# A recurrence between two expert FFNs: beats of up to five steps, copies moved to ScalarE, another bank and another plan

## The chip, the cores and the metric

The kernel runs on one core of a Trainium2 chip. The metric is the device time of one execution in microseconds (us). The core has a matmul engine (TensorE, PE in the profile; PEld is its weight load), VectorE (DVE), ScalarE (ACT), GpSimd (POOL) and a queue engine (SyncE, SP) that issues most of the plain DMAs. GpSimd issues the indirect DMAs.

## The reference

Input x is 16 sequences of 512 tokens of 128 numbers, float32. Three stages, each with a residual:

```python
x = x + 0.5 * ffn(layernorm(x), router_w, expert_fc, expert_proj)
x = x + rnn(layernorm(x), Wi, bi, Wh, bh)
x = x + 0.5 * ffn(layernorm(x), router_w, expert_fc, expert_proj)
```

`rnn` is a recurrence over the 512 tokens of each sequence: h = tanh(xi[t] + h @ Wh.T + bh), with xi = x @ Wi.T + bi. `ffn` sends every token to one of 8 experts, the argmax of its 8 logits; the expert computes square(relu(x @ fc)) @ proj.T with 512 hidden units.

## The kernel before, in words

**Units, tiles, steps.** The 512 time steps are cut into 16 units of 32 (UNIT). A unit has 512 tokens, 4 rows of 128 (UR). Both FFNs gather tokens by expert into tiles of 128 tokens. The first FFN has two groups (FIRST = [4, 12] units): 23 tiles and 55 tiles. The second FFN has one pool of 71 tiles, which is filled in stages of SECOND = [7, 3, 3, 1, 1, 1] units; a tile can be loaded when its stage is routed and scattered, and the last 18 of the 71 wait for the last stage. A step t needs state t-1 (`step`, L1632, two 16-column matmuls on PE; `tanh`, L1441, on ACT), so the 512 steps are one chain.

**One tile.** Its rows arrive in `xs_sb` (`fetch`, an indirect DMA of POOL at L1085, in the first FFN; `load`, SP, L968, in the second), its expert's weights in `w_sb` (`weights`, SP, L980). PE transposes it (`turn_x`, L1600), ACT copies the result (`copy_x`, L1456), PE makes the hidden units in two halves of four matmuls (`product1`, L1609), DVE applies relu (`relu`, L1334), ACT squares in two halves (`square`, L1449), PE multiplies back in two halves (`product2`, L1622) into the bank `yp`. DVE takes it from there in `finish`: a plain copy in the first FFN (L1344), a scaled addition in the second (L1341). Results of the first FFN go to DRAM (`store`, SP, L985) and come back row by row (`gather`, POOL, L1110); those of the second are put in place by POOL (`put`, L1116). After each indirect DMA POOL clears a small buffer (L1137).

**Unit by unit.** What a unit needs before its steps: `gather` 4 rows, `add_back` (L1352), statistics (L1161, L1165), a root on POOL (L1058, L1061), `normalise` (L1184), a transposition `turn2` on PE whose result ACT evacuates (L1472), `inputs` (`xi`, L1591) into bank z[u % 2], `add_bias` (L1359). After its steps: `hadd` (a transposition that DVE adds up, L1364), `turn` (a transposition that ACT evacuates), `logits` (L1547). A stage then has `pick`, `rank` (L1559), `place` and `list` on DVE and PE, and its rows are scattered to DRAM by POOL (`scatter`, L1094).

**Routing of the first FFN.** For each group `logits`, `pick`, `rank`, `slots`; then a list of tokens is made by matmuls of one-hot matrices (`hot` by DVE or POOL, L1073; `index`, L1580) and copied out (`table`, L1287). The bank of group 0 is z[0], that of group 1 is z[1]; therefore `xi` of unit 0 waits for table 0 and `xi` of unit 1 for table 1.

**The order of the work.** Nothing is decided on the chip: `plan` simulates the kernel in Python with costs and arrival times written in it (ARRIVE, PR) and writes a list of beats. A beat has at most one tile in each of its three phases (transposition of the next, first product of the present, second product of the last), up to BEAT = 4 steps, up to two turns, and side work on PE and DVE. Each engine runs its part of the beats in this fixed order. On PE a beat is: step 0, turn_x, first half of product 1, first turn, step 1, second half of product 1, half of logits or xi, step 2, half of product 2, second turn, step 3, the other half of product 2, the other half of logits or xi, then rank and index. On ACT: tanh 0, square, tanh 1, square, evacuation of the first turn, tanh 2, copy_x, tanh 3, evacuation of the second turn. When a beat has no tile, PE fills up with matmuls whose result nobody reads (`keep_warm`, L1637).

`centre` (8 products at the start, L1530) subtracts the mean from the experts' first weights; ACT writes the result back and SP stores it to `fc_dram`, from which all tiles' weights come.

## Time and profile before

| | us |
|---|---|
| median of 3 runs | 615.17 |
| lowest and highest of them | 611.65, 615.24 |
| the profiled execution's own time | 610.88 |
| its span, first to last instruction | 609.2 |
| PE busy in the span | 557.5 |
| ACT busy in the span | 232.0 |

The span is what the profile divides up; the time of the same execution is 1.7 us longer. The profile's busy PE includes the matmuls of `keep_warm`.

### The profile page before, as it was taken

What the parts mean: (1) busy time and instruction counts of PE and PEld (TensorE: products, weight loads), DVE (VectorE), ACT (ScalarE), POOL (GpSimd) and SP (SyncE); (2) the same over time, 40 slices, a digit from 0 to 9 for tenths busy, and PEclk for the clock granted to TensorE, in tenths of its full rate; (3) what the DMA queues carried; (4) which work ended last, traced back from release to release, by engine and by line L of the source; (5) the groups of instructions that cost most, each with busy time, mean ns of one, the idle gap of its engine ahead of it and who ended that gap; (6) DMA issues with size and microseconds to landing.
All of it is one profiled execution on the core that took longest, in us unless ns stands there. A gap on an engine that the chain in (4) does not pass through costs nothing.

```text
span 609.2 us, 14909 instructions
## 1 busy us (share of the span) xinstructions
PE 557.5 (92%) x4503; PEld 521.0 (86%) x4503; DVE 338.7 (56%) x1169; ACT 232.0 (38%) x950; POOL 443.4 (73%) x637
## 2 busy tenths in 40 slices
PE   7978979979999999999999999899999899997992
PEld 6677877979999899998998888889999899896991
DVE  3617889565564455545468511645647774675550
ACT  1203321334445444454442433344454444433440
POOL 3486089887756878887857898877774878778672
PEclk9997999999999999999999999999999999999997
DMA  7976850254434444444411013544343354445740
GB/s 278 400 247 201 257 170 7 39 176 137 142 112 139 124 135 132 141 127 120 110 41 58 31 41 101 162 127 135 123 140 113 99 149 153 123 152 159 222 129 1
DMA packets 58476, 83.07 MB, mean 136 GB/s; under 512 B 10031, under 2 KB 30386, under 8 KB 57888
## 3 DMA queue, kind: packets, MB, share of 16 engines
q1 hardware_dynamic: 49392, 64.20, 33.2%
q0 software_dynamic: 8864, 17.78, 10.1%
q8 instruction: 40, 0.66, 0.4%
q14 instruction: 36, 0.29, 0.2%
q10 hardware_dynamic: 144, 0.14, 0.1%
HBM read 65.81 MB, written 16.72 MB: 135 GB/s over the span
## 4 chain that ended last, share of the span: by engine, by line
PE 71%; DVE 10%; issue 7%; POOL 5%; DMA 2%; ACT 2%; SPq 1%; ACTq 1%; POOLq 0%; DVEq 0%
PE yp L1622 20%; PE hp L1609 16%; PE z L1632 14%; PE hp L1637 7%; PE mT L1508 4%; POOL out_dram L1116 3%; PE xTp L1600 2%; PE lg L1547 2%; PE z L1591 2%; PE z L1580 2%; DVE r_sb L1334 1%; POOL hot L1073 1%; DMA hsT<-in_x_rows_dram 1%; PE z L1547 1%; DVE stats L1161 1%
## 5 line engine op out<-in xcount | busy, mean ns | idle before, releaser
L1622 PE MATMUL yp<-projT,s_sb 128*128 x1192 | 192.0, 292 | 23.0 <-DVE y_sb L1344 7.6
L1441 ACT ACTIVATE hsT<-z 128x16 f32<-128x16 f32 x512 | 93.8, 183 | 242.2 <-PE z L1632 181.3
L1609 PE MATMUL hp<-xT_sb,w_sb 128*128 128x128 f32 x1192 | 182.7, 283 | 0.5 <-ACT xT_sb L1456 0.5
L1632 PEld LDWEIGHTS z<-hsT,w_all 128*128 128x128 f32 x1024 | 155.3, 190 | 29.5 <-ACT hsT L1441 7.2
L1622 PEld LDWEIGHTS yp<-projT,s_sb 128*128 128x128 f32 x1192 | 154.3, 193 | 27.9 <-issue 27.5
L1334 DVE TENSOR_SCALAR r_sb<-hp 128x512 f32<-128x512 f32 x149 | 102.7, 689 | 120.8 <-PE hp L1609 87.4
L1632 PE MATMUL z<-hsT,w_all 128*128 128x16 f32 x1024 | 159.9, 232 | 7.2 <-ACT hsT L1441 4.9
L1609 PEld LDWEIGHTS hp<-xT_sb,w_sb 128*128 128x128 f32 x1192 | 157.0, 195 | 1.0 <-ACT xT_sb L1456 0.7
L1449 ACT ACTIVATE s_sb<-r_sb 128x256 f32<-128x256 f32 (+1 forms) x247 | 112.0, 454 | 75.1 <-issue 45.6
L1137 POOL MEMSET idle<- 128x400 f32 x277 | 125.2, 452 | 0.2
L1110 POOL DMA_INDIRECT back<-ys_dram,pos x64 | 62.0, 969 | 49.3 <-DMA ys_dram<-y_sb 23.8
L1116 POOL DMA_INDIRECT out_dram<-y_sb,xs_sb x71 | 69.6, 980 | 29.9 <-issue 17.2
L1085 POOL DMA_INDIRECT xs_sb<-in_x_rows_dram,index x78 | 75.8, 972 | 15.3 <-issue 11.5
L1094 POOL DMA_INDIRECT xs_dram<-pay,pos x64 | 62.7, 979 | 21.7 <-DVE pos L1297 12.0
L1637 PE MATMUL hp<-w_all,ident 128*128 128x256 f32 x178 | 59.1, 418 | 0.0
L1456 ACT ACTIVATE xT_sb<-xTp 128x128 f32<-128x128 f32 x149 | 40.5, 272 | 16.9 <-issue 9.7
L1600 PE MATMUL xTp<-ident,xs_sb 128*128 128x128 f32 x149 | 44.4, 298 | 0.5 <-ACT xT_sb L1456 0.5
L1344 DVE COPY y_sb<-yp 128x128 f32<-128x128 f32 x78 | 22.1, 283 | 25.2 <-PE yp L1622 20.6
L1341 DVE SCALAR_TENSOR_TENSOR y_sb<-yp,xs_sb 128x128 f32<-128x128 f32 x71 | 24.6, 347 | 20.5 <-PE yp L1622 15.5
L1073 POOL TENSOR_SCALAR hot<-kio,slot_f,ids 128x128 f32<-128x128 f32 x28 | 23.8, 860 | 15.4 <-DVE slot_f L1257 15.4
L1600 PEld LDWEIGHTS xTp<-ident,xs_sb 128*128 128x128 f32 x149 | 29.4, 197 | 1.0 <-DMA xs_sb<-xs_dram 1.0
L1161 DVE BATCH_NORM_STATS2 stats<-pay 128x6 f32<-128x128 f32 x128 | 27.7, 280 | 0.5
(154 smaller groups left out, 483.2 us busy)
## 6 DMA issues: line engine op xcount, KB each, us to landing
w_sb<-fc_dram SPq DMA_DIRECT2D x149, 256.0 KB
ys_dram<-y_sb SPq DMA_DIRECT2D x78, 64.0 KB
xs_sb<-xs_dram SPq DMA_DIRECT2D x71, 65.0 KB
hsT<-in_x_rows_dram SPq DMA_DIRECT2D x16, 256.0 KB, 4.3
hsT<-in_x_cols_dram SPq DMA_DIRECT2D x3, 1024.0 KB, 16.3
fc_sb<-in_fc_in_dram SPq DMA_DIRECT2D x4, 512.0 KB, 5.4
projT<-in_proj_in_dram SPq DMA_DIRECT2D x1, 2048.0 KB, 11.6
fc_dram<-fc_sb SPq DMA_DIRECT2D x8, 256.0 KB
```

What stands on the lines that cost most here:

```text
L1085: pool.indirect_dma_start(out=xs_sb[:, g % RING, 0:D], out_offset=None, in_=x_rows.rearrange("p (n d) -> (p n) d", d=D), in_offset=bass.In ...
L1094: pool.indirect_dma_start(out=xs2_dram, in_=pay[:, n, :], in_offset=None, out_offset=bass.IndirectOffsetOnAxis(ap=pos[:, 1, n:n + 1].bitca ...
L1116: pool.indirect_dma_start(out=out.rearrange("b t d -> (b t) d"), in_=y_sb[:, g % RING, :], in_offset=None, out_offset=bass.IndirectOffsetO ...
L1137: pool.memset(idle[:, :], 0.0).then_inc(s_idle, 1)
L1334: dve.tensor_scalar(r_sb[:, g % 2, :], hp[:, g % 2, :], 0.0, None, ALU.max).then_inc(s_relu, 1)
L1441: act.activation(state(t), z_step(t), ACT.Tanh).then_inc(s_h, 1)
L1449: act.activation(s_sb[:, g % 2, half * w:(half + n) * w, :].rearrange("p c t -> p (c t)"), r_sb[:, g % 2, half * w * P:(half + n) * w * P] ...
L1600: pe.transpose(xTp[:, 0:P], xs_sb[:, g % RING, XR:XR + D], ident[:, :]).then_inc(s_tx, 1)
L1609: mm = pe.matmul(hp[:, g % 2, h * P:(h + 1) * P], w_sb[:, g % WRING, h * P:(h + 1) * P], xT_sb[:, g % 2, :], start=True, stop=True)
L1622: mm = pe.matmul(yp[:, 0:D], s_sb[:, g % 2, h, :], projT[:, bass.ds(offsets[g] + h * D, D)], start=(h == 0), stop=(h == HC - 1))
L1632: pe.matmul(z_step(t), WhT, state(t - 1) if t else hsT[:, 0:B], start=False, stop=True, skip_group_check=True).then_inc(s_mm, 1)
L1637: pe.matmul(lg[:, 0:FILL] if early else hp[:, 0, 0:FILL], ident[:, :], w_all[:, 0:FILL], start=True, stop=True)
```

## The change

- BEAT is 5. A fifth step may be in a beat only for steps from PR["from"] = 89.4 to PR["to"] = 402.9; elsewhere a beat has at most four. PE does step 4 after the second half of product 2 and the second half of logits or xi. ACT does tanh 4 as its last tanh.
- Turns move: a lone turn, or the second of two, is now done by PE at the end of the beat behind step 4, and evacuated by ACT as the last thing of the beat; the first of two stands where the second stood.
- The first FFN's copy out of `yp` goes from DVE (`finish`) to ACT (`bring`), behind tanh 3 and copy_x and ahead of tanh 4. There are two semaphores (s_y1, s_y2) in place of s_y, and `made` waits on the one of the tile's kind.
- Group 1 of the first FFN uses the bank `lg`, that the second FFN's logits use; the second FFN's first stage waits for table 1 before its first logits, and `xi` of unit 1 no longer does. The early `keep_warm` writes to the free half of `xTp`.
- `centre` pieces are exempt from the planner's limits on room in a beat, so that they come in a row; the planner takes the first weights as ready 5.2 us after the last of them (4.0 before), and the rows of x as arriving 5 to 5.5 us later.
- SECOND is [7, 1, 1, 3, 1, 1, 1, 1], eight stages for six. The last stage is the same.
- All of the planner's weights (PR) are other numbers, so the order of beats, of SP's queue and of POOL's queue is another.

```diff
-BEAT = 4
+BEAT = 5
-SECOND = [7, 3, 3, 1, 1, 1]
+SECOND = [7, 1, 1, 3, 1, 1, 1, 1]
-          ... "rows": [34.0 + 1.2 * u for u in range(FIRST[0])] + [45.0 + 2.0 * u for u in range(NU - FIRST[0])]}
-PR = {"lat1": 317.13, "lat2": 230.174, "lat3": -30.24, "last": -472.607, "hor": 65.326, "beat": 1.723, "put": -120.179, "dve": 2.508, "act": 0.415, "pe": -0.984, "early": 2.791, "load": 0.767, "hold": -207.944, "late": -122.862, "gather": -278.073, "scatter2": 505.514, "fetch": -278.424, "slack": -26.428}
+          ... "rows": [39.5 + 1.2 * u for u in range(FIRST[0])] + [50.0 + 2.0 * u for u in range(NU - FIRST[0])]}
+PR = {"lat1": 255.575, "lat2": 265.398, "lat3": -19.271, "last": -329.665, "hor": 127.118, "beat": 5.85, "put": -103.734, "dve": 3.048, "act": 4.178, "pe": 0.886, "early": 5.706, "load": -0.726, "hold": -85.01, "late": -170.227, "gather": -260.2, "scatter2": 637.695, "fetch": -55.443, "slack": 59.124, "from": 89.418, "to": 402.858}
...
-            at = max(choice[1], ev["centre", E - 1] + 4.0, ...
+            at = max(choice[1], ev["centre", E - 1] + 5.2, ...
-        while t < T and len(b.steps) < BEAT and ...
+        while t < T and len(b.steps) < (BEAT if PR["from"] <= t < PR["to"] else BEAT - 1) and ...
-                if d_pe and pe_at + d_pe > pe_room and (b.pe or b.turns) or d_act and ...
+                if what != "centre" and d_pe and pe_at + d_pe > pe_room and (b.pe or b.turns) or what != "centre" and d_act and ...
...
-            return lg[:, :] if r.second else z[:, r.index, :]
+            return z[:, 0, :] if r.index == 0 else lg[:, :]
...
+            def bring(g):
+                act.wait_ge(s_m2, g + 1)
+                if g >= RING:
+                    put_landed(act, g - RING)
+                act.activation(y_sb[:, g % RING, :], yp[:, 0:D], ACT.Copy).then_inc(s_y1, 1)
...
                         if last is not None and i < 2:
                             square(last, i, 1)
-                        if i == 1:
-                            if turns[0]:
-                                evacuate(*turns[0])
+                        if i == 3 and len(turns) > 1 and turns[0]:
+                            evacuate(*turns[0])
                         if after is not None and i == 2:
                             copy_x(after)
-                    if turns[1]:
-                        evacuate(*turns[1])
+                        if last is not None and not is_second[last] and i == 3:
+                            bring(last)
+                    if turns and turns[-1]:
+                        evacuate(*turns[-1])
...
-                    if u < len(first):
-                        pe.wait_ge(s_table, table_no[first[u].index])
+                    if u == 0:
+                        pe.wait_ge(s_table, table_no[first[0].index])
...
-                if b.turns:
-                    turn(b.turns[0])
-                elif alone and n > 0:
+                if alone and n > 0:
                     keep_warm()
...
                 if alone and n > 3 and not products:
                     keep_warm()
+                if n > 4:
+                    step(b.steps[4])
+                if b.turns:
+                    turn(b.turns[-1])
+                elif alone and n > 4:
+                    keep_warm()
```

## Rows read from the trace of the kernel before

**Rows 1.** The page, busy time by engine: us, share, instructions.
```profile
PE 557.5 (92%) x4503; PEld 521.0 (86%) x4503; DVE 338.7 (56%) x1169; ACT 232.0 (38%) x950; POOL 443.4 (73%) x637
```

**Rows 2.** Stretch, length, busy PE, PEld, DVE, ACT, POOL; clock, DMA share, GB/s.
```profile
125.30:137.80 12.50, 9.38 (x72) 8.18 (x72) 8.99 (x35) 3.60 (x8) 11.08 (x17) 1.00 0.66 201
137.80:320.00 182.20, 176.37 (x1493) 169.94 (x1493) 95.95 (x316) 85.57 (x384) 136.01 (x195) 1.00 0.41 122
320.00:384.00 64.00, 64.00 (x437) 52.32 (x434) 26.96 (x110) 20.60 (x101) 55.15 (x78) 1.00 0.21 67
384.00:534.80 150.80, 142.10 (x1235) 137.50 (x1236) 91.63 (x295) 68.65 (x312) 114.07 (x161) 1.00 0.42 131
...
562.30:597.20 34.90, 33.92 (x298) 33.52 (x298) 18.40 (x36) 14.09 (x34) 24.23 (x35) 1.00 0.55 163
```

**Rows 3.** Stretch, length, busy (count), clock, DMA: ACT at L1441 alone: one instruction for each step.
```profile
137.80:320.00 182.20, 38.82 (x212) 1.00 0.41 122
320.00:384.00 64.00, 17.04 (x93) 1.00 0.21 67
384.00:534.80 150.80, 32.08 (x175) 1.00 0.42 131
```

**Rows 4.** The same, DVE at L1334 alone: one instruction for each tile.
```profile
137.80:320.00 182.20, 37.21 (x54) 1.00 0.41 122
384.00:534.80 150.80, 30.05 (x44) 1.00 0.42 131
```

**Rows 5.** The same, PE at L1637 alone: the filling matmuls.
```profile
320.00:384.00 64.00, 46.88 (x140) 1.00 0.21 67
```

**Rows 6.** Timeline of ACT, beats with a tile: start, us, instruction, [idle before].
```profile
140.09 0.18 ACT L1441 ACTIVATE hsT<-z 128x16 f32<-128x16 f32 x1 [0.32 <-issue]
140.76 0.18 ACT L1441 ACTIVATE hsT<-z 128x16 f32<-128x16 f32 x1 [0.49 <-PE z L1632]
...
153.62 0.18 ACT L1441 ACTIVATE hsT<-z 128x16 f32<-128x16 f32 x1 [0.52 <-PE z L1632]
...
154.76 0.18 ACT L1441 ACTIVATE hsT<-z 128x16 f32<-128x16 f32 x1 [0.65 <-issue]
...
155.15 0.59 ACT L1472 ACTIVATE xnT<-mT 128x512 f32<-128x512 f32 x1
155.62 0.18 ACT L1441 ACTIVATE hsT<-z 128x16 f32<-128x16 f32 x1
```

**Rows 7.** Timeline of DVE and PE in the same two beats.
```profile
140.69 0.29 DVE L1344 COPY y_sb<-yp 128x128 f32<-128x128 f32 x1 [0.51 <-PE yp L1622]
...
153.99 0.60 PE L1508 MATMUL mT<-ident,xn 128*128 128x128 f32 x4
154.43 0.29 PE L1632 MATMUL z<-hsT,w_all 128*128 128x16 f32 x2
154.57 0.69 PE L1609 MATMUL hp<-xT_sb,w_sb 128*128 128x128 f32 x4
```

**Rows 8.** Timeline of the start: centring, a statistics wait, the first gather.
```profile
18.70 1.02 PE L1530 MATMUL hp<-fc_sb,level 128*128 128x512 f32 x2
...
19.99 1.02 PE L1530 MATMUL hp<-fc_sb,level 128*128 128x512 f32 x2
...
26.91 1.02 PE L1530 MATMUL hp<-fc_sb,level 128*128 128x512 f32 x2
...
44.47 0.87 DVE L1161 BATCH_NORM_STATS2 stats<-hsT 128x6 f32<-128x128 f32 x4 [5.92 <-DMA hsT<-in_x_rows_dram]
...
78.00 0.95 POOL L1110 DMA_INDIRECT back<-ys_dram,pos  x1 [22.18 <-DMA ys_dram<-y_sb]
```

**Rows 9.** Timeline from the last gather of unit 1 to its bias.
```profile
118.86 0.95 POOL L1110 DMA_INDIRECT back<-ys_dram,pos  x1 [0.17 <-issue]
...
136.72 0.76 DVE L1359 TENSOR_SCALAR z<-z,bias 128x512 f32<-128x512 f32 x1 [0.69 <-PE z L1591]
```

**Rows 10.** Timeline of POOL and SP: first scatter of the second FFN, first load.
```profile
323.28 1.02 POOL L1094 DMA_INDIRECT xs_dram<-pay,pos  x1 [2.02 <-DVE pos L1297]
...
374.80 0.30 SPq L968 DMA_DIRECT2D xs_sb<-xs_dram  x1
```

More of the change, by code:

```diff
@@ L365, in possible @@
         if what == "xi":
-            if key < len(first) and ("table", first[key]) not in ev:
+            if key == 0 and ("table", first[0]) not in ev:
                 return None
@@ L470, in on_pe @@
             if alone and n > 3 and not products:
+                warm()
+            if n > 4:
+                yield from step(4)
+            if b.turns:
+                yield from turn(len(b.turns) - 1)
+            elif alone and n > 4:
                 warm()
@@ L506, in evacuate, with bring @@
                     do(0.59, p)
+            def bring():
+                yield ("m2", last), ("free", last - RING) if last >= RING else None
+                do(0.26, ("y", last))
+            by_act = last is not None and order[last][0] is not None
             if n > 0:
@@ L544, in end @@
                 do(0.292, ("y", last))
-            if last is not None and not n:
+            by_dve = last is not None and order[last][0] is None
+            if by_dve and not n:
                 yield from end()
@@ L555, in on_dve @@
                 do(dve_time(p), p)
-            if last is not None and n:
+            if by_dve and n:
                 yield from end()
@@ L594, in plan @@
         after = line.pop(0) if line and ev.get(("load", line[0]), 1e9) <= pe + PR["load"] and ev["w", line[0]] <= pe + PR["load"] + 1.0 else None
-        while t < T and len(b.steps) < BEAT and ev.get(("bias", t // UNIT), 1e9) <= pe + 0.3:
+        while t < T and len(b.steps) < (BEAT if PR["from"] <= t < PR["to"] else BEAT - 1) and ev.get(("bias", t // UNIT), 1e9) <= pe + 0.3:
             b.steps.append(t)
@@ L647, in plan @@
                         lg_after[lg_owner] = lg_last
-                elif what == "place":
+                elif what == "place" or what == "table" and piece[1].index:
                     lg_owner, lg_last = None, piece
@@ L917, in put_landed, with made @@
             engine.wait_ge((s_put if is_second[g] else s_store)[g % RING], 16 * n)
+        def made(engine, g):
+            n = sum(is_second[i] == is_second[g] for i in range(g + 1))
+            engine.wait_ge(s_y2 if is_second[g] else s_y1, n)
         def offset(engine, kind, g):
@@ L1426, in _ @@
                     add_states(*p[1:])
-                if last is not None and not b.steps:
+                if last is not None and is_second[last] and not b.steps:
                     finish(last)
@@ L1430, in _ @@
                     side(p)
-                if last is not None and b.steps:
+                if last is not None and is_second[last] and b.steps:
                     finish(last)
@@ L1475, in _ @@
                 after, last = tile_at(b.at + 1), tile_at(b.at - 1)
[L1476 removed]
+                turns = [p if p[0] != "hadd" else None for p in b.turns]
                 if b.steps:
```

59 lines of the change are left out of this document (32 added, 27 removed).

## The prediction, made before the change was run

> **What bounds the kernel now.** I began with the page's busy times: PE is busy 557.5 of 609.2 us [rows 1], which looks like a kernel bound by PE. The table of stretches says something else [rows 2]. From 320 to 384 us PE is busy all the time, but 46.88 of its 64 us are filling matmuls [rows 5]: there is no tile to work on, and only the recurrence advances. So I cut the span by what the recurrence does, with the count of tanh instructions in each stretch [rows 3].
>
> The chain of steps runs without a break from about 97.6 us to 532.4 us (the last tanh). Its parts: 32 steps up to 125.3; a stop of 12.5 us with no step; 212 steps in 182.2 us (0.86 us each, 54 tiles beside them [rows 4]); 93 steps in 64.0 us (0.69 each, no tile); 175 steps in the next 148.4 us (0.85 each, 44 tiles beside them). After the last step come about 30 us in which the last unit is routed and scattered, 34.9 us for the 18 tiles of the last stage (1.94 us each [rows 2]) and 12.0 us in which the last results land and the program ends. The sum is 97.6 + 27.7 + 12.5 + 182.2 + 64.0 + 148.4 + 76.8 = 609.2, the span. So the end is set by the start of the recurrence, by its steps, and by a tail of 76.8 us that no faster PE shortens, as long as enough tiles are done when the steps end. It is by this sum that I cost the change.
>
> Inside a beat with a tile, tanh follows tanh after 0.67 us (140.09 to 140.76 [rows 6]), and in beats without a tile after 0.69 us on average with all their side work. So a half product of four matmuls between two steps costs the chain nothing: it fills PE while the chain goes through ACT. What costs is everything beyond it. A turn in the first gap makes 1.14 us of one interval and 0.86 of the next (153.62, 154.76, 155.62 [rows 6]), 0.47 + 0.19 = 0.66 us in all. turn_x costs about 0.1 us a tile. Each half of logits or xi costs about what the four matmuls of a turn cost, 0.44 us (153.99 to 154.43 [rows 7]).
>
> **Part by part.**
>
> *Start (to the first step, 97.6 us).* The centring products come every 1.3 us (18.70, 19.99) and then wait; the eighth is at 26.91 [rows 8]. In a row it would come 2.6 us after the sixth, at about 22.6: 4.3 us earlier for the first weights. Their store shares the DMA queues with the first loads and may not gain as much: I take 3. DVE waits 5.92 us for rows of x with the relu of a tile behind it [rows 8]; with the later arrival in the plan these statistics stand later: 2 us. The copies of the first 11 tiles leave DVE (0.29 us each, 0.2 of it not overlapped): 2 us, as the first gather, which waited 22.18 us for stores [rows 8], starts that much earlier. Together 7 us, bounds 0 and 11.
>
> *The stop before unit 1 (12.5 us).* The new bank takes away the wait of `xi` for table 1. But the trace shows that the data was late too: the last gather of unit 1 is issued at 118.86, its bias done at 137.5 [rows 9]. POOL, with hots and fetches in its queue, decides when those gathers come. PR still gives hots precedence. I take half of the stop, 6 us; bounds 0 and 12.5.
>
> *Fifth step and moved turns.* The fifth step makes no step faster by itself: the interval is 0.67 with a half product or without. What changes is the turn. Behind step 4 PE has nothing to do until the state is back, so a turn that DVE evacuates (hadd) costs nothing there: 0.44 us saved. One that ACT evacuates starts 0.14 us after step 4's own matmuls start; the evacuation can start 0.69 later (0.60 of matmuls and the signal) and gives ACT free 0.47 later (155.15 to 155.62), so the next tanh can start 1.30 us after step 4. Without the turn it would start at 0.33 (154.43 to 154.76) + 0.67 = 1.00. Cost 0.30 for 0.66. A unit has one turn of the first and two of the second kind: 0.44 + 2 x 0.36 = 1.2 us saved a unit. In beats of four steps the turn follows a half product: 0.83 for 0.66, 0.34 a unit lost. By my count of steps in the new order, 8.2 units run beside tiles in beats of five and 5.2 in beats of four: -9.8 + 1.8 = -8.0 us. Bounds -12 (the 0.66 wholly gone) and +4 (the plan makes few full beats of five).
>
> *The copy on ACT.* In the trace DVE starts it at 140.69 and the next tanh starts at 140.76 [rows 6, 7]. On ACT I take the 0.29 us that it has on DVE, less the 0.12 by which the next instruction there starts before the end of one (155.15 + 0.59 against 155.62): the tanh would start at 140.86 instead, 0.10 us late. Queued behind the waiting copy are that tanh, hence all later steps, and the evacuation. The 55 tiles of group 1 run beside steps: +5.5 us, the 23 of group 0 mostly do not. Bounds 0 (where logits or xi stand between) and 0.5 us a copy, 27 us: the wait for product 2 then holds a tanh for most of a period.
> The Trainium skill (Perfetto Trace Analysis, Optimizing Scalar/DVE Operations) says that if DVE is saturated, work may be moved to ScalarE. The trace does not show DVE saturated: DVE is busy 56% over the span, and ACT, at 38% [rows 1], is the engine that the chain passes through; by the rule alone the 55 copies would be a gain, by the rows they cost 5.5 us.
>
> *Fewer tiles a step, and the scatter.* With five steps to a tile, step 224, which opens the first stage of seven units, comes with about 42 instead of 48 of the 55 tiles done, and the remaining 13 fill part of the 51.5 us that the 28 scatters and the rest of POOL's queue take from 323.28 to the first load at 374.80 [rows 10]. The stretch without tiles shrinks from 64 to some 35 us. For the chain this is no gain: the same 95 or so tiles are done before it ends, and 1.3 units more run beside tiles, where their side work is not free (0.6 for turns and 1.76 for logits and xi a unit): +3 us. Bounds 0 and +8.
>
> *Two more stages.* Some 5 us of DVE each beside relu; DVE has 59 us free from 384 to 534.8 [rows 2]. +1, bounds 0 and +4.
>
> *Tail.* The last stage is the same, 18 tiles: 0. About 40 tiles of the second FFN are done at the last step as before; each one fewer below that costs 1.94 us. Bounds -3 and +8.
>
> Sum: -7 - 6 - 8.0 + 5.5 + 3 + 1 = -11.5, a span of 597.7 us and a time of 599.4 for an execution like the profiled one (1.7 more). The three runs shown lie 0.8 to 4.4 us above the profiled one; with their middle, 2.6, I forecast 602.
>
> **The rivals.**
>
> *A. PE's work decides after all.* Then what counts is the filling that goes: the stretch without tiles loses 29 of its 64 us, PE spent 73% of it on filling, so 21 us come off, and with 4 of the start 25: 609.2 - 25 + 1.7 + 2.6 = 588. For it: 92% busy. Against it: the tail starts from the last step, however early tiles were done. It needs the steps to end some 20 us earlier, thus 0.81 instead of 0.86 us beside tiles, which the free turns alone do not give.
> This is also what the Trainium skill would make of it (Perfetto Trace Analysis, Optimization Strategies): the goal is to keep the matmul engine at high utilization. Here PE is fully busy in a stretch where it does little of use.
>
> *B. ScalarE becomes the chain's bound, slower.* The place is the copy in front of tanh 4 (or the next beat's tanh 0) and the late evacuation. The gains without the copy sum to 17 us; over 55 copies they are gone when a copy holds the next tanh by 0.31 us on average. At 0.5 us it is 27.5 - 17 = +10.5: 609.2 + 10.5 + 4.3 = 624. For it: a wait for product 2 is now ahead of a tanh, 55 times. Against it: ACT is only 38% busy, and DVE's copy could start 0.07 us before the tanh did.
>
> *C. The change does not do what it says.* The stop stays, since unit 1's gathers come behind hots and stores (0 for -6), the start gains 3, the rest cancels (-8 + 5.5 + 3 + 1 = +1.5): a span of 607.7, a time of 612.
>
> **How the numbers follow.** Forecast 0.45, A 0.2, C 0.2, B 0.15. About 1% is what a measurement of this kernel can tell from no change, 6 us here: faster means below 609.0, slower above 621.3. Faster: most of the forecast (0.38), all of A (0.2), a little of C (0.04), 0.62. Slower: two thirds of B and a little of the forecast's bad bounds, 0.12. The rest, 0.26, is no change. The range goes from A's 588 less 1 to C's 612 plus the 5 of the stages' and the tail's bad bounds: 587 to 617.
>
> **What would show it.** The start: first tanh near 90.6. Unit 1: the stop between steps 32 and 33 about 6 us. Beside tiles: five tanh to a square pair, 0.84 us or a little less a step; a turn interval near 0.97 in place of 1.14 and 0.86. The copy: a tanh behind it 0.10 us late. The stretch with filling matmuls: about 35 us. The distance from the last tanh to the end: 77 us. Wrong would be: a tail longer than 80 us, steps beside tiles above 0.87 us, or PE idle in front of step 4.

## The result, and the profile after

| | before | after |
|---|---|---|
| median, us (20 runs each, same chip) | 614.99 | 612.88 |
| lowest, highest | 611.65, 617.0 | 606.4, 637.64 |
| the profiled execution's span | 609.2 | 616.3 |

The ratio is 0.9929, interval 0.9903 to 0.9954: 0.7% faster, inside the 1% that the prediction called no change. It leaves out seven slow executions of the changed kernel (617.99 us and more); the medians of all 20, as in the table, differ by 0.3%. The forecast was 602, the range 587 to 617. The time lies next to rival C's 612, but C's reason ("the change does not do what it says") is only half of it. The executions of the changed kernel scatter far more than those of before and go with their granted clock: those at 0.983 to 0.989 took 606.4 to 610.2 us, those at 0.975 to 0.978 took 612.2 to 615.4, those at 0.964 to 0.968 took 618.0 to 620.6. The profiled one (617.99 us, 0.967) is one of the last.

The page of the changed kernel: busy time, as in [rows 1], and the granted clock in 40 slices of the span.

```profile
PE 561.1 (91%) x4459; PEld 525.9 (85%) x4459; DVE 334.3 (54%) x1149; ACT 251.1 (41%) x1024; POOL 442.8 (72%) x637
PEclk9988999999999999999997899699999999999998
```

The busy line is nearly that of before. The clock line is not: around the 22nd and the 26th slice, 330 and 390 us, it falls.

The stretches of the changed kernel, cut at its own steps (after step 32, 256, 320 and the last), columns as in [rows 2]; then tanh alone, as in [rows 3].

```profile
125.60:137.10 11.50, 9.51 (x75) 8.62 (x75) 8.31 (x29) 4.43 (x13) 10.25 (x16) 1.00 0.70 212
137.10:320.90 183.80, 176.89 (x1514) 170.00 (x1514) 90.76 (x289) 98.40 (x441) 147.59 (x210) 1.00 0.44 122
320.90:373.60 52.70, 51.05 (x306) 42.80 (x306) 27.77 (x109) 17.02 (x80) 44.26 (x63) 0.87 0.21 65
373.60:536.00 162.40, 152.58 (x1249) 145.92 (x1249) 90.55 (x303) 71.14 (x324) 111.14 (x158) 0.96 0.41 118
```
```profile
137.10:320.90 183.80, 41.03 (x225) 1.00 0.44 122
320.90:373.60 52.70, 11.77 (x65) 0.87 0.21 65
373.60:536.00 162.40, 35.30 (x192) 0.96 0.41 118
```

Steps beside tiles did get faster (183.80 / 225 = 0.817 us against 0.86 in [rows 3]), and steps with few or no tiles got slower (52.70 / 65 = 0.81 against 0.69), at a mean clock of 0.87.

The same cut for all kernels below that matter. The columns are times of tanh instructions in each trace (us from the span's start), except the stop, the gap between the tanh of steps 32 and 33. The rows from b_fill on are of another chip, on which the kernel before takes 600 and not 615 us; compare within one chip. "b_fill" stands there for the kernel before (it takes the same time, see below).

| | first | stop | step 97 | step 225 | step 321 | last | span |
|---|---|---|---|---|---|---|---|
| before | 97.8 | 13.0 | 189.4 | 302.9 | 372.5 | 532.4 | 609.2 |
| after | 98.5 | 11.5 | 190.5 | 290.9 | 373.6 | 535.8 | 616.3 |
| b_fill | 98.0 | 13.3 | 188.8 | 296.1 | 365.3 | 521.0 | 598.8 |
| e_fill5 | 98.5 | 11.4 | 188.3 | 287.5 | 362.7 | 516.7 | 596.6 |
| b_turns | 96.4 | 17.2 | 191.9 | 299.4 | 374.3 | 531.2 | 607.9 |
| b_copy | 97.3 | 12.9 | 186.7 | 292.5 | 361.6 | 517.0 | 593.3 |

So the start gained nothing, the stop 1.5 us; the units from step 97 to 224 gained 13 us; and all of it was given back by step 321. Not all of that is one cause: from step 225 to 321 the changed kernel takes 82.7 us, its filled version e_fill5 75.2, before 69.6 and b_fill 69.2. So some 7.5 of the 13 us go with the filling that e_fill5 adds, and some 6 stay with it. From step 321 to the last, after takes 162.2 us and e_fill5 154.0, another 8. (On one chip, again and e_fill differ by 1.1 and 10.1 us in these two stretches; again had its long fall later, see below.)

### The profile page after: what moved, and what is told of

The parts are those of the page before. It is cut to its first block, busy times and chain, and to the rows that moved or that the text cites. A ratio compares the mean times of both kernels' runs of the same rounds, so it can differ in the third digit from the quotient of the medians.

```text
span 616.3 us, 14886 instructions
## 1 busy us (share of the span) xinstructions
PE 561.1 (91%) x4459; PEld 525.9 (85%) x4459; DVE 334.3 (54%) x1149; ACT 251.1 (41%) x1024; POOL 442.8 (72%) x637
## 4 chain that ended last, share of the span: by engine, by line
PE 75%; issue 6%; DVE 6%; DMA 5%; POOL 4%; ACT 2%; SPq 0%; POOLq 0%; DVEq 0%; ACTq 0%
PE yp L1649 20%; PE hp L1636 18%; PE z L1659 14%; PE hp L1664 6%; PE mT L1533 4%; PE lg L1574 3%; PE xTp L1627 3%; POOL out_dram L1136 3%; PE z L1618 2%; DMA fc_dram<-fc_sb 2%; DVE r_sb L1354 1%; PE lg L1607 1%; POOL idle L1157 1%; PE z L1574 1%; ACT hsT L1458 1%
## 5 line engine op out<-in xcount | busy, mean ns | idle before, releaser
L1659 PEld LDWEIGHTS z<-hsT,w_all 128*128 128x128 f32 x1024 | 161.5, 196 | 34.8 <-ACT hsT L1458 14.8
L1659 PE MATMUL z<-hsT,w_all 128*128 128x16 f32 x1024 | 164.7, 237 | 12.7 <-ACT hsT L1458 8.0
L1649 PEld LDWEIGHTS yp<-projT,s_sb 128*128 128x128 f32 x1192 | 155.6, 195 | 22.2 <-issue 21.6
L1636 PEld LDWEIGHTS hp<-xT_sb,w_sb 128*128 128x128 f32 x1192 | 158.9, 198 | 2.7 <-issue 2.5
L1136 POOL DMA_INDIRECT out_dram<-y_sb,xs_sb x71 | 69.6, 980 | 51.6 <-DVE y_sb L1360 34.0
L1664 PE MATMUL hp<-w_all,ident 128*128 128x256 f32 x136 | 48.4, 443 | 0.0
L1479 ACT ACTIVATE y_sb<-yp 128x128 f32<-128x128 f32 x78 | 21.6, 278 | 51.4 <-PE yp L1649 40.5
```

The source lines that it names most:

```text
L1136: pool.indirect_dma_start(out=out.rearrange("b t d -> (b t) d"), in_=y_sb[:, g % RING, :], in_offset=None, out_offset=bass.IndirectOffsetO ...
L1636: mm = pe.matmul(hp[:, g % 2, h * P:(h + 1) * P], w_sb[:, g % WRING, h * P:(h + 1) * P], xT_sb[:, g % 2, :], start=True, stop=True)
L1649: mm = pe.matmul(yp[:, 0:D], s_sb[:, g % 2, h, :], projT[:, bass.ds(offsets[g] + h * D, D)], start=(h == 0), stop=(h == HC - 1))
L1659: pe.matmul(z_step(t), WhT, state(t - 1) if t else hsT[:, 0:B], start=False, stop=True, skip_group_check=True).then_inc(s_mm, 1)
L1664: pe.matmul(xTp[:, P:P + FILL] if early else hp[:, 0, 0:FILL], ident[:, :], w_all[:, 0:FILL], start=True, stop=True)
```

## The experiments

**Where half of the 13 us goes, and 8 us more behind step 321: the clock.** Windows around the two falls, in the changed kernel; then PE's timeline and ACT's.

```profile
326.00:330.00 4.00, 3.18 (x27) 2.89 (x25) 3.69 (x19) 1.74 (x8) 3.51 (x6) 1.00 0.21 66
330.00:343.50 13.50, 13.50 (x55) 12.09 (x55) 8.10 (x36) 2.90 (x14) 9.24 (x14) 0.51 0.18 55
388.50:402.00 13.50, 12.95 (x63) 12.74 (x62) 4.96 (x17) 3.79 (x19) 7.15 (x10) 0.50 0.25 70
```
```profile
328.48 0.40 PE L1659 MATMUL z<-hsT,w_all 128*128 128x16 f32 x2 [0.27 <-issue]
329.15 0.39 PE L1659 MATMUL z<-hsT,w_all 128*128 128x16 f32 x2 [0.27 <-issue]
329.81 0.40 PE L1659 MATMUL z<-hsT,w_all 128*128 128x16 f32 x2 [0.27 <-ACT hsT L1458]
```
```profile
335.32 0.18 ACT L1458 ACTIVATE hsT<-z 128x16 f32<-128x16 f32 x1 [1.10 <-PE z L1659]
336.60 0.18 ACT L1458 ACTIVATE hsT<-z 128x16 f32<-128x16 f32 x1 [1.10 <-PE z L1659]
```

At 328 us a tile is in its last phase only. Such an edge beat gets no filling matmuls, as `keep_warm` fills only beats without any tile: PE does a step's two small matmuls and idles 0.27 us, three times in a row. From 330 us the granted clock is 0.5 (1.2 GHz) for 13.5 us, and tanh follows tanh after 1.28 us in place of 0.67. The same happens at 388.5, behind three such idle times from 385.55 on. The Trainium skill (TensorE: Matmul & The Clock Gate, HAM oscillation) tells of long waits of PE for DMA as what brings the low clock; this trace does not agree: no wait in the 4 us before either fall was longer than 0.27 us.

What the fifth step has to do with it shows in a kernel with at most four steps and no filling, e_four (below). PE in its edge beat at the end of the first FFN:

```profile
306.59 0.40 PE L1659 MATMUL z<-hsT,w_all 128*128 128x16 f32 x2 [0.27 <-ACT hsT L1458]
307.26 0.40 PE L1659 MATMUL z<-hsT,w_all 128*128 128x16 f32 x2 [0.27 <-ACT hsT L1458]
```

Here, and in the kernel before (317.31, 317.98), two such idle times follow each other and not three, and the granted clock is 1.00 from 60 to 590 us. The beat of five adds the third. Not every beat with three brings a fall: e_dvecopy (below) has one at 342.18, with a fall at 344.9, and one at 395.80, without.

*again*: the changed kernel unchanged. *e_fill* and, in a later session, *e_fill5*: with filling matmuls in edge beats too. *b_fill*: the kernel before with the same.

```diff
-                if alone and n > 0:
-                    keep_warm()
+                if now is None and n > 0:
+                    keep_warm(False, *other)      (likewise in the other gaps without a product)
```

Expected of again: 

> The kernel after, unchanged, for a second profile. Theory 1 (the granted clock falls where a beat has one tile in one phase only and PE is not filled): a profile in which those falls are missing or shorter has a span near 606 us, and the stretches around 330 and 390 us are shorter by 5 us each. Rival (the falls are a disturbance from outside that any kernel has): they stand at other places, or the kernel before of the same call has them too.

Expected of e_fill: 

> The kernel after with the filling matmul also in beats in which only one phase has a tile; the plan is the same, every output is computed. Theory 1: the granted clock stays at full speed from 320 to 410 us, the time is 604 to 608 us in every run and no run lies above 612. Rival (the fill costs chain time or the falls have another cause): the times still spread from 606 to 620, or all of them are longer by some us.

Expected of e_fill5: 

> The changed kernel with filling matmuls also in beats that have a tile in one phase only, once more, in five rounds. Theory (the filling removes the spells of half clock and nothing else): 0.985 to 0.997 of the time before, and the profile's granted clock 0.5 nowhere between 300 and 420 us. Rival (the gain was that of one chip): 1.00 or above.

Expected of b_fill: 

> The kernel before, its order of work kept, with the same filling matmuls in beats that have a tile in one phase only. Theory (the missing filling hurts the changed kernel alone, since the kernel before leaves its edge beats at full clock in its trace): 0.995 to 1.005 of the time before. Rival (the filling is worth as much there, and nothing of what it gave is the change's): 0.985 to 0.99.

| | us | ratio to before, same chip |
|---|---|---|
| again | 608.45 | 1.0116 [1.0059, 1.0173] |
| e_fill | 597.99 | 0.9972 [0.9952, 0.9991] |
| e_fill5 | 599.64 | 0.9983 [0.9959, 1.0008] |
| b_fill | 600.47 | 0.9993 [0.9971, 1.0016] |

On the two chips of this table (again and e_fill on one, e_fill5 and b_fill on the other) the kernel before takes 599.6 and 600.6 us, and the changed one is 1.2% slower. The filling takes 10.5 us off it, and nothing off the kernel before. In the trace of again the clock falls behind the same two edge beats, at 328.8 for 3.4 us and at 380.0 for 23.9; so the rival (a disturbance from outside) is not borne out, and neither is my hope for a profile without falls. The executions of again spread from 604.3 to 613.2 us, those of e_fill from 595.7 to 600.4. My 604 to 608 for e_fill was missed because I had it from the first chip's times; e_fill5's 0.9983 lies just outside the 0.985 to 0.997 expected of it. The windows of e_fill5, over the same times:

```profile
330.00:343.50 13.50, 13.45 (x82) 10.31 (x82) 7.63 (x30) 4.17 (x21) 11.31 (x17) 1.00 0.14 46
388.50:402.00 13.50, 12.18 (x106) 11.72 (x105) 8.42 (x32) 5.76 (x27) 11.55 (x17) 1.00 0.39 112
```

The clock is 1.00 and PE is no busier than before; it only has 82 and 106 matmuls where there were 55 and 63. So the falls are shown to come from edge beats without filling. The filling does not keep every fall away: in e_stages (below), filled too, the clock falls at 399.9 for 6.8 us, behind a wait of PE of 2.00 us. Most of the kernels below are filled, so that the change's other parts can be read; where one is not, the text says so.

**The fifth step.** *e_four*: at most four steps in a beat, order made anew, no filling. *e_fourfill*: the same with filling.

```diff
-"from": 89.418, "to": 402.858}
+"from": 1e9, "to": 1e9}
```

Expected of e_four: 

> The kernel after with at most four steps in every beat; all other edits and weights stay, so the plan is made anew. If the fifth step and the free turns behind it made the steps faster: steps 96 to 224 take 108 to 113 us (before 113.5, after 100.4), and step 224 comes 8 to 12 us later than 290.9. If it was the other weights of the plan: they take 100 to 104 us here too. The whole: 608 to 614, because what is gained up to step 224 was lost again by step 320 in the kernel after.

Expected of e_fourfill: 

> The changed kernel with at most four steps in a beat (the order is made anew) and the filling matmuls. Theory (a fifth step is worth some 1.2 us a unit over the units that run beside tiles in such beats, and what it brings is kept once the clock holds): 3 to 6 us slower than the same kernel with five. Rival (the beats of five bring nothing at the end, since the steps saved are given back where no tile is): equal within 1.5 us. The run without the filling was at 1.010 of before on its chip, against 1.012 with five steps.

e_four took 605.89 us, 1.0099 [1.0070, 1.0127]; e_fourfill 607.39, 1.0138 [1.0098, 1.0177], against e_fill5's 0.9983 beside it. With filling the fifth step is worth 1.3% to 1.5%, 8 to 9 us, more than the 3 to 6 that I expected. Without filling it is worth nothing: e_four took 605.9 us and again 608.5 on the same chip, with intervals that overlap. From step 97 to 224 e_fourfill takes 104.2 us and e_fill5 99.2: 1.25 us a unit. Both carry the moved turns, so the prediction's terms make it 1.2 + 0.34 = 1.54. e_four takes 104.1 us there, not the 108 to 113 that I expected of it, against 113.5 before and 107.3 in b_fill: a part of the 13 us is the new order and the copy, and not the fifth step.

**The moved turns and the copy, each alone in the kernel before, its order of work kept, without filling.** *b_turns* moves the turns, *b_copy* gives ScalarE the first FFN's copy.

```diff
 b_turns, on PE (ScalarE likewise)
-                if b.turns:
-                    turn(b.turns[0])      (behind step 0)
+                if b.turns:
+                    turn(b.turns[-1])     (end of the beat; the first of two behind step 2)
 b_copy, on ScalarE
+                    if last is not None and not is_second[last]:
+                        bring(last)       (behind the fourth tanh; gone from DVE)
```

Expected of b_turns: 

> The kernel before, its order of work kept, in which a lone turn or the second of two stands at the end of the beat on PE and last on ScalarE, the first of two where the second stood. Theory (with four steps in a beat the moved turn stands behind a half product): an interval with such a turn is 1.1 to 1.5 us in place of 1.17 and 0.86, nothing is gained, 0.998 to 1.006 of before. Rival (the moved turns by themselves are what made units 3 to 6 shorter): 0.99 or less.

Expected of b_copy: 

> The kernel before, its order of work kept, with the first FFN's copy out of the bank yp on ScalarE, behind the fourth tanh of a beat and copy_x. Theory (the tanh behind a copy is late by no more than some hundredths of a us, and DVE's queue no longer holds the copy back): 0.985 to 1.000 of before. Rival (my term, 0.10 us for each of 55 copies on the chain): 1.009. Rival (the copy's wait for the product holds the next tanh): above 1.01.

b_turns took 612.39 us, 1.0218 [1.0184, 1.0252]; b_copy 594.51, 0.9915 [0.9886, 0.9944]. The moved turns alone cost 12 us, three times what I had allowed them at worst, and more than the 0.998 to 1.006 that I expected of the run; the copy alone gains 5.5 us, as expected of it, and gives the fastest kernel of this study.

The profiled execution of b_turns is its fastest (609.61 us), 9.1 us longer than that of b_fill. None of it is lost beside tiles: steps 193 to 224 take 25.66 us in b_turns and 25.58 in b_fill (a lone moved turn makes one interval of 1.47 or 1.11 us, an unmoved one 1.17 to 1.30, and 0.86 behind it if ACT evacuates it). It is lost in two places that I had not costed. One is the stop before unit 1, 17.2 us for 13.3: there the turns are in a chain (hadd, turn, turn2 of unit 1), and each now stands behind a tile's two products. The other is the tile-free units, steps 257 to 320: 48.5 us for 42.9. ACT in b_turns and then in b_fill:

```profile
330.98 0.18 ACT L1441 ACTIVATE hsT<-z 128x16 f32<-128x16 f32 x1 [0.48 <-PE z L1630]
331.94 0.60 ACT L1472 ACTIVATE xrt<-mT 128x512 f32<-128x512 f32 x1 [0.78 <-PE mT L1506]
332.43 0.18 ACT L1441 ACTIVATE hsT<-z 128x16 f32<-128x16 f32 x1
```
```profile
325.73 0.18 ACT L1441 ACTIVATE hsT<-z 128x16 f32<-128x16 f32 x1 [0.49 <-PE z L1632]
325.81 0.59 ACT L1472 ACTIVATE xrt<-mT 128x512 f32<-128x512 f32 x1
326.40 0.18 ACT L1441 ACTIVATE hsT<-z 128x16 f32<-128x16 f32 x1
```

In b_fill the evacuation fits between two tanh, 0.67 us apart: a turn in the first gap of a beat without a tile is free. Moved to the end, the evacuation waits for PE and the next tanh waits behind it, 1.45 us.

The copy is free where I charged 0.10 us. The changed kernel's ACT, beats of five with a tile, and at 323.50 one with a copy and a turn:

```profile
307.60 0.18 ACT L1458 ACTIVATE hsT<-z 128x16 f32<-128x16 f32 x1 [0.32 <-PE z L1659]
308.14 0.28 ACT L1479 ACTIVATE y_sb<-yp 128x128 f32<-128x128 f32 x1 [0.36 <-PE yp L1649]
...
311.46 0.18 ACT L1458 ACTIVATE hsT<-z 128x16 f32<-128x16 f32 x1 [0.32 <-PE z L1659]
312.00 0.28 ACT L1479 ACTIVATE y_sb<-yp 128x128 f32<-128x128 f32 x1 [0.36 <-PE yp L1649]
312.18 0.18 ACT L1458 ACTIVATE hsT<-z 128x16 f32<-128x16 f32 x1
```
```profile
323.50 0.28 ACT L1479 ACTIVATE y_sb<-yp 128x128 f32<-128x128 f32 x1 [0.28 <-PE yp L1649]
323.70 0.18 ACT L1458 ACTIVATE hsT<-z 128x16 f32<-128x16 f32 x1
324.18 0.60 ACT L1495 ACTIVATE xrt<-mT 128x512 f32<-128x512 f32 x1 [0.30 <-issue]
324.68 0.18 ACT L1458 ACTIVATE hsT<-z 128x16 f32<-128x16 f32 x1
```

The tanh behind a copy starts at 311.46 + 0.72, 0.05 us late, and the next interval is 0.05 shorter: in b_copy they read 0.72 and 0.69 where b_fill has 0.67 and 0.73. The turn behind step 4 makes 323.70 to 324.68 = 0.98 us, as predicted (0.97). *e_dvecopy* puts the copy of the changed kernel, its order kept, back on DVE, without the filling.

```diff
-                        if last is not None and not is_second[last] and i == 3:
-                            bring(last)
+                    dve.tensor_copy(y_sb[:, g % RING, :], yp[:, 0:D]).then_inc(s_y1, 1)     (in finish)
```

Expected: 

> The kernel after with the first FFN's copy out of the second product's bank back on DVE, in DVE's old place in the beat; the plan is the same. Theory of the prediction (each copy on ACT holds the next tanh by 0.10 us): steps 96 to 224 take 2 to 3 us less than the 100.4 us of the kernel after, the whole 3 to 5 us less. Rival (the copy fits in a gap of ACT): no difference from 96 to 224, and the start is later by 1 to 3 us, as DVE has the copies of group 0 again.

It took 618.91 us, 1.0269 [1.0222, 1.0316], 10.5 us more than again. The first tanh is at 103.6 for 101.1, the stop 15.0 us for 11.5, the gap at step 256 5.3 for 3.9: the copy on DVE holds back what the recurrence waits for in the stops. That is not all: from step 97 to 224 it takes 103.2 us for 99.2, where the theory had 2 to 3 us less and the rival no difference, so both were wrong there. In b_copy against b_fill 2.1 us are gained by step 97, 0.4 of it in the stop, and 1.5 from 97 to 224. That DVE's queue is the reason is argued from these places; no run here shows which operation on DVE was held up.

**Another order of work, and the stages.** *e_oldplan*: the filled code with the planner's weights and six stages of before, no fifth step. *e_stages*: only the six stages. *e_tablewait*: the filled kernel in which `xi` of unit 1 waits for table 1 again. *before_again*: the kernel before, looked at on the chip of the last two.

```diff
 e_oldplan: PR of before;  e_oldplan and e_stages
-SECOND = [7, 1, 1, 3, 1, 1, 1, 1]
+SECOND = [7, 3, 3, 1, 1, 1]
 e_tablewait
-                    if u == 0:
-                        pe.wait_ge(s_table, table_no[first[0].index])
+                    if u < 2:
+                        pe.wait_ge(s_table, table_no[first[u].index])
```

Expected of e_oldplan: 

> The filled changed code with the planner's weights and the six stages of before, and no fifth step. Theory (the new order of work carries the difference to four steps with the new weights, 1.014): 1.00 to 1.01 of before. Rival (the code's edits cost what they cost whatever the order): 1.014 or above.

Expected of e_stages: 

> The filled kernel after with SECOND = [7, 3, 3, 1, 1, 1], six stages as before; the plan is made anew with the same weights. The prediction gave the two more stages 1 us of cost: the whole 0 to 2 us faster. Rival (the smaller stages bring tiles earlier): 2 to 6 us slower, with PE filled for longer after step 350.

Expected of e_tablewait: 

> The filled kernel after in which unit 1's inputs wait for table 1 again, as they had to while the index of group 1 stood in their bank; the plan is the same. Theory (the bank held nothing up, the gathers did): stop 11.4 us as without the wait, whole within 1 us. Rival (the bank's wait was part of the stop): the stop grows by 1 us or more and so does the whole.

Expected of before_again: 

> The kernel before, unchanged, for a profile beside the others. In the last comparison it took 599.6 us where it took 615.0 in the first, and the kernel after was 1.2% slower than it instead of 0.7% faster. Theory 2 (the first comparison held waits of the kernel before that are absent here): its steps 64 to 320 take less than the 187 us that they took in the first profile, by some 10 us, mostly around steps 96 to 224. Rival (the start is what differs): its first step comes some 10 us before 97.8.

e_oldplan took 612.8 us, 1.0228 [1.0193, 1.0263], with a gap of 15.9 us at step 128: the theory (1.00 to 1.01) fell, but so large a gap says that the old weights do not suit the new code, and I learn little more from it than that the order has to be made for the code. On a chip where before takes 612.12 us, before_again took 616.77: from step 64 to 320 210.5 us, where the first profile had 208.7 (the 187 of the expectation is not what that trace shows). So this chip was no test of why the kernel before takes 600 us elsewhere. There e_stages took 610.08, 0.9955 [0.9921, 0.9989], and e_tablewait 605.49, 0.9869 [0.9809, 0.9929]. The eight stages are worth 4.6 us and not -1: with six there are gaps of 3.3 and 3.1 us at steps 352 and 360, and from step 225 to 361 they cost 5.9 us against e_tablewait. The fall of the clock at 399.9, just behind them, adds 1.5 us up to step 370. The intervals of the two ratios overlap slightly, so the size is uncertain. The wait for table 1 makes no difference to the stop, 11.5 us with it and 11.4 without (e_fill5, on another chip; the filled kernel did not run on this one): the bank that the change freed held nothing up.

**What the stop before unit 1 waits for.** In the changed kernel, from the last gather of unit 1 to its bias (POOL, DVE and PE in order of time):

```profile
118.21 0.95 POOL L1130 DMA_INDIRECT back<-ys_dram,pos  x1 [0.17 <-issue]
```
```profile
125.45 1.13 DVE L1369 SCALAR_TENSOR_TENSOR pay<-back,scales,hsT 128x128 f32<-128x128 f32 x4
...
130.81 1.49 DVE L1204 TENSOR_SCALAR xn<-pay,mv,rstd 128x128 f32<-128x128 f32 x4
...
135.05 0.76 DVE L1376 TENSOR_SCALAR z<-z,bias 128x512 f32<-128x512 f32 x1 [0.18 <-PE z L1618]
```
```profile
132.36 0.66 PE L1533 MATMUL mT<-ident,xn 128*128 128x128 f32 x4 [1.28 <-DVE xn L1204]
...
133.98 1.03 PE L1618 MATMUL z<-xnT,w_all 128*128 128x256 f32 x4
```

The add stands in DVE's order behind the table and a relu, 6 us behind the last gather's end; the chain behind it takes 10 us more. It is the order, of POOL and then of DVE. Two kernels change it: *e_gather1* gives unit 1's gathers the precedence of unit 0's on POOL; *e_unit1* does that and puts unit 1's pieces ahead of the routing of group 1 on every engine.

```diff
-            if p[1][2] == 0:
+            if p[1][2] <= 1:
                 return -1900
 e_unit1 alone
-            return (owner.u0 * UNIT - t) * 0.66 - PR["lat3"] if owner.u0 else -850
+            return (owner.u0 * UNIT - t) * 0.66 - PR["lat3"] if owner.u0 > 1 else -850
```

Expected of e_gather1: 

> The filled kernel after, with unit 1's gathers given the precedence that unit 0's have in the plan of GpSimd's queue. Theory (the stop after step 32 is there because unit 1's gathers come late, whatever bank the index has): the stop of 11.4 us falls below 4, step 64 comes 5 to 9 us earlier, the whole is 2 to 8 us faster than the filled kernel. Rival (something else holds unit 1): the stop stays above 9.

Expected of e_unit1: 

> The filled kernel with unit 1's four gathers and its pieces on every engine ahead of the routing of group 1. Theory (the stop before unit 1 is made by the order, and the steps saved wait at step 128 for the results of group 1's first tiles): no stop over 2 us at step 32, a stop of over 8 us at step 128, which comes no earlier than 214 us; the whole at 0.995 to 1.03 of before. Rival (the stop is worth its 11.5 us): step 128 some 10 us earlier and the whole at 0.97 to 0.98.

e_gather1 (on the chip of e_stages) took 622.49 us, 1.0150 [1.0077, 1.0222]. My expectation failed: the stop stayed at 12.1 us, since PE's turn of unit 1 remained behind the index products (its rows were normalised by 118 and turned at 139), and a stop of 14.3 us came up at step 128. e_unit1 took 626.97, 1.0427 [1.0385, 1.0469], above the 1.03 that I allowed it: the stop at step 32 is 1.6 us, as meant, and step 128 is reached at 210.6, before my 214 and only 1.2 us earlier than in e_fill5 (211.8), though the stop is 9.8 us shorter. There stands a gap of 25.3 us, and one of 15.0 at step 160. POOL in e_unit1, at the first gather of unit 4:

```profile
208.10 0.95 POOL L1130 DMA_INDIRECT back<-ys_dram,pos  x1 [19.61 <-issue]
```

When unit 4 starts, 49 to 53 tiles are done, in every order that I ran. In a stop tiles run undisturbed (2.6 us each in that of e_unit1, against 3.5 beside five steps); if the steps do not stop before unit 1, they stop at step 128, where POOL stands 19.61 us in front of unit 4's first gather. So in the orders tried the stop is mostly slack of the chain of tiles and not a loss that a wait less would give back; both orders also delay tiles (the 23rd relu is at 137.5 and 135.6 us for 128.0 in e_fill5), and one that shortens the stop without that was not tried.

**The start.** The chain of waits of the changed kernel:

```profile
20.05 0.87 PE hp L1555 x2
20.93 0.02 issue
20.95 0.61 ACT fc_sb L1495
21.55 0.02 issue
21.57 11.38 DMA fc_dram<-fc_sb
```

and of the kernel before:

```profile
28.60 4.57 DMA fc_dram<-fc_sb
33.18 0.47 SPq L928
```

In PE's timeline the last centring product now comes at 19.89 and not at 26.91 [rows 8], even earlier than I said. Its store lands at 32.95 all the same, and at 33.17 before: the DMA queues are nearly full until then (share 0.95 before and 0.92 after from 20 to 33 us, and 0.66 before from 33 to 40). *e_norow* puts the last two centring products back late in the filled kernel, which moves no other work.

```diff
+    for e, at in ((6, 20), (7, 25)):
+        beats[9 + e].turns, beats[at].turns = [], [("centre", e)]
```

Expected: 

> The filled changed kernel, of whose centring products the last two come late again, one among the index products and one behind them, about where they stood before. Theory (the stores of the centred weights land at 33 us because the DMA queues are full of the first loads, whenever they are issued before 27 us): first tanh within 0.7 us of the filled kernel's 98.5 to 100, the same time within 1.5 us. Rival (my term: the centring in a row is worth 3 us and something else lost it): first tanh 3 us later.

597.45 us, 0.9961 [0.9938, 0.9984], first tanh at 97.8. The last product came at 30.19, even later than in the kernel before, and its store was issued at 31.87, behind the 27 us of the theory; the first weights were loaded 1 us later (34.55 for 33.61) and nothing was lost by it: the row of centring products was worth nothing.

**Towards a faster version.** *e_turnsback*: the filled kernel with the turns back in their old places in beats of up to four steps. *e_turnsback2*: also in beats of five without a tile.

```diff
-                if b.turns:
+                if late and b.turns:       (late: n > 4;  in e_turnsback2: n > 4 and not alone)
                     turn(b.turns[-1])
```

Expected of e_turnsback: 

> The filled changed kernel, its order of work kept, in which the turns of beats with at most four steps stand where the kernel before had them (the first behind step 0, the second behind step 2); only beats of five have them at the end. Theory (the moved turns cost the chain in the units without tiles and in the stops, and are free only beside five steps): units 8 and 9 together 43 to 44 us in place of 46.2, the stop before unit 1 shorter by 1 us or more, 0.980 to 0.992 of before. Rival (the order was made for the moved turns, and loses elsewhere what it gains there): 0.995 to 1.005.

Expected of e_turnsback2: 

> As the kernel with the turns taken back in beats of four, and also in beats of five without a tile: only beats of five with a tile have a turn at the end. Theory (a turn behind step 0 of a beat without a tile is free, one at its end costs 0.30 us): no interval of 0.97 us in units 8 and 9, these two together 44.5 to 45.5 us in place of 46.2, 1 to 3 us less in all, 0.990 to 0.998 of before. Rival (the time there is bound by the scatters and not by the steps): units shorter, the whole unchanged or longer tail.

e_turnsback took 599.16, 0.9980 [0.9955, 1.0006]: too little, where its rival had it. The stop was 0.9 us shorter, but units 8 and 9, which I had taken for beats of four, are beats of five, and a turn behind the fifth step there still made 0.98. e_turnsback2 took 595.91, 0.9943 [0.9922, 0.9963]; units 8 and 9 take 45.4 us for 46.2. b_copy stays the fastest here, with the order of before; their intervals overlap.

## Why the prediction was wrong, point by point

- **Start, -7.** Failed: 0.7 us later. The step that failed is "Their store shares the DMA queues with the first loads and may not gain as much: I take 3". It gained 0.2. With the first weights no earlier, no gather was: the first comes at 77.91 for 78.00, so the 2 us for the copies and the 2 for the statistics did not show either. On the changed kernel the copies do count, 2.5 us in e_dvecopy.
- **Stop, -6.** 1.5 us came off. I had seen that gathers come late, and still took half for the bank; e_tablewait shows the bank worth nothing, e_unit1 that the stop is slack of the tiles.
- **Fifth step and moved turns, -8.0.** A turn behind the fifth step was sized right (0.98 us for 0.97), and five steps against four nearly (1.25 us a unit for 1.54). What failed is the place: I costed turns beside tiles only. In tile-free units they had been free and cost 0.30 behind a fifth step and 0.78 behind a fourth; in the stops they lengthen a chain. Alone, in the kernel before, they are +12 us.
- **The copy, +5.5.** Wrong sign: -5.5. The tanh behind it is 0.05 late and catches up, and, with the copy gone from DVE's queue, the recurrence comes sooner in the stops and beside tiles, though DVE is busy only 56% [rows 1]. The Trainium skill (Perfetto Trace Analysis, Optimizing Scalar/DVE Operations) has the move for a saturated DVE. That condition was not met here, and the move paid all the same; what decided was not the busy share.
- **Fewer tiles, +3.** The term that failed most. "For the chain this is no gain ... +3 us" prices only the side work of 1.3 units; the clock stands at nothing in it, without a reason. I asked what filling costs and not what it does: three unfilled gaps in an edge beat of five bring the low clock, 10.5 us (again against e_fill, one chip). On that chip the changed kernel is 8.9 us slower than before where I had 11.5 faster, so the clock is half of the error of 20.4; on the first chip the change took 2.1 us off where I had 11.5. A further 6 us from step 225 to 321 stay with filling: 3.3 in the tile-free units (the turns), the rest before them, with a stop of 3.9 us at step 256 that the kernel before does not have; I did not look for its cause. The tile-free stretch, said to shrink to 35 us, is 59 (relu at 326 to relu at 385; 70 before by the same reading), and 52 in e_fill: with a first stage of seven units, the 28 scatters still take from 316.8 to 364.7.
- **Stages, +1.** Wrong sign, -4.6: six stages leave gaps in the steps that eight close.
- **Tail, 0.** +3.7 (80.5 us), past the 80 that I had named as a sign of being wrong; in e_fill5 +2.1 over b_fill. The step that failed is "About 40 tiles of the second FFN are done at the last step as before": 121 of the 149 relu stand before the last tanh in the kernel before and 119 in the changed one. Two tiles more at the prediction's 1.94 us are 3.9. Windows of the tail, after and then before:

```profile
585.00:600.00 15.00, 15.00 (x137) 15.00 (x137) 8.16 (x17) 6.37 (x16) 10.96 (x17) 1.00 0.47 138
```
```profile
578.00:593.00 15.00, 15.00 (x136) 15.00 (x135) 8.08 (x17) 6.36 (x16) 11.11 (x17) 1.00 0.47 143
```

  PE is busy all the time, POOL for 11 of 15 us, and in both kernels a put is issued every 1.89 us on average: a tile costs the same as before, there are more of them. I tried no kernel for this, but the traces agree: the tail is 76.2 to 78.0 us in the six traces with 121 tiles at the last tanh and 79.4 to 81.3 in the eleven with 119. More than 121 give no more, since the last stage's 18 must wait: 77.4 with 124 (e_four).
- **Rivals.** A (588) fell: steps beside tiles did reach 0.817 us, but the steps did not end earlier (535.8 for 532.4), as A needs. B fell by b_copy. C's number was near (612 for 612.88), and that is luck: its reason was nearly right for the stop (0 for 1.5), for the start it still had a gain of 3, and for the rest it was wrong. Gains of 13 us in the middle met losses of as much by step 321, about 7.5 by the clock and 6 by turns and a stop, and the tail's 3.7.
- **The sum.** The last step from a profiled execution to a forecast adds 2.6 us, the middle of 0.8 and 4.4; the median of the three runs lies 4.3 above it, which makes 603.7 and not 602.

Filled, on one chip (e_fill5 against b_fill, spans), the change reads: start +0.5, stop -1.9, the rest up to step 97 +0.9, steps 97 to 224 -8.1, 225 to 320 +6.0, 321 to the last -1.7, tail +2.1; -2.2 in all, where the prediction had -11.5. So the forecast would have failed without the clock too.

What stays open: the kernel before takes 0.86 us a step beside tiles in its profile here and 0.82 in b_fill on the faster chip, where the filling had changed nothing. Single intervals of 0.67 us become 0.8 to 1.6, at granted clock 1.00, and before those that I looked at the profile names only the step's own matmuls; the changed kernel shows hardly any of it (99.8 us from step 97 to 224 in e_tablewait, 99.2 in e_fill5). With it goes that the change, once filled, is worth 1.3% on the chip of e_tablewait and 0.2% on that of e_fill5. The cause is not known, and no run was made for it.

## What to carry to other kernels

A filler that is there to keep the clock up is to be checked in the beats in which the real work is thin, not only in the empty ones: two unfilled gaps in a row brought no low clock here, and a change that made them three did, in most executions. When a change makes thin beats longer or shifts them, look at the granted clock slice by slice before anything else. The price of moving an operation is read in every kind of stretch it occurs in (beside work, without work, in a stop), since it may be free in one and the whole chain in the next. And a stop is worth its length only if nothing else, here 49 tiles before step 128, is waiting to become the next stop.

## What the runs showed of the hardware that I had not expected

- The granted clock fell to 0.50 for 13.5 us with PE busy 3.18 of the 4.00 us before it, no idle time over 0.27 us. It fell so twice in the changed kernel and twice in again, each time behind three such idle times, and not in e_four or before, with two in a row. In e_dvecopy three of them brought it once and once not.
- A 256 KB store issued at 21.6 us lands after 11.4 us, one issued at 28.6 after 4.6 us: both at 33. One issued at 31.87 (e_norow) held the first weight load up by 1 us only.
- One kernel (before) takes 600, 612 or 615 us by the chip, and two kernels do not shift alike: the changed one took 0.7% less than it on one chip and 1.2% more on another.
